# Routing with three chunks in flight and shares in the scattered rows; expert results added into the output by an indirect, accumulating DMA

## The reference

```python
h = x + _attention(_rmsnorm(x, ln1_w), wq, wk, wv, wo)
h = h + _moe(_rmsnorm(h, ln2_w), gate_w, w1, w2, w3)
# _moe:
logits = xf @ gate_w.T
rw, sel = jax.lax.top_k(logits, 2)
rw = jax.nn.softmax(rw, axis=-1)
for e in range(E):
    we = jnp.sum(jnp.where(sel == e, rw, 0.0), axis=-1)
    hid = jax.nn.silu(xf @ w1[e].T) * (xf @ w3[e].T)
    out = out + hid @ w2[e].T * we[:, None]
```

## Time and profile before

| | us |
|---|---|
| median of three runs (3338.06 to 3340.56) | 3339.76 |
| profiled execution, its time | 3338.2 |
| its span | 3336.7 |
| PE busy | 2885.8 (86%) |
| DVE busy | 2463.1 (74%) |
| ACT busy | 1954.1 (59%) |
| POOL busy | 1090.8 (33%) |

### The profile page before, as it was taken

One profiled execution on the slowest core, in us unless ns is written; L12 is line 12 of the kernel. 1 busy time (PEld: TensorE's weight loads), 2 busy tenths in 40 slices (PEclk: granted clock), 3 DMA queues, 4 the chain that ended last, 5 costly groups with the idle time before them and its releaser, 6 DMA issues. The chain is left out here.

```text
span 3336.7 us, 48301 instructions
## 1 busy us (share of the span) xinstructions
PE 2885.8 (86%) x14320; PEld 1233.6 (37%) x14321; DVE 2463.1 (74%) x2747; ACT 1954.1 (59%) x3515; POOL 1090.8 (33%) x652
## 2 busy tenths in 40 slices
PE   5798998889877758999999999999999963899990
PEld 1234434334323431222222222222222252899980
DVE  0599999999998558888888888888888365233323
ACT  3566656655643325888787878787887810344430
POOL 1788779778773450000000000000000036100107
PEclk8899999999998877999999999999999975999995
DMA  1111111111110542111111111111111036111114
GB/s 43 39 51 43 46 54 48 42 54 51 39 44 22 161 144 39 39 37 37 35 39 39 39 40 39 36 32 35 30 38 35 1 118 249 50 47 47 47 41 150
DMA packets 123096, 185.29 MB, mean 56 GB/s; under 512 B 30224, under 2 KB 77968, under 8 KB 122896
## 3 DMA queue, kind: packets, MB, share of 16 engines
q1 hardware_dynamic: 109072, 142.95, 15.0%
q0 software_dynamic: 13824, 39.86, 3.8%
HBM read 138.01 MB, written 44.43 MB: 55 GB/s over the span
## 5 line engine op out<-in xcount | busy, mean ns | idle before, releaser
L1529 DVE TENSOR_REDUCE nmh<-ring 128x2 f32<-128x1024 f32 x1024 | 1196.0, 1219 | 196.1 <-PE ring L1406 195.9
L1387 ACT ACTIVATE prob<-s_ps 128x512 f32<-128x512 f32 x2048 | 1072.9, 602 | 282.5 <-PE s_ps L1427 282.5
L767 DVE TENSOR_TENSOR_SCAN h<-dA,state,bx 128x512 f32<-128x512 f32 x512 | 618.9, 1269 | 124.7 <-ACT dA L606 124.6
L391 POOL TENSOR_TENSOR bx<-u,bb 128x2048 f32<-128x2048 f32 x128 | 578.9, 4527 | 198.1 <-DVE h L767 198.0
L1427 PE MATMUL s_ps<-qs,ks 98*128 98x512 bf16 x2048 | 613.9, 387 | 17.2 <-issue 11.5
L1439 PE MATMUL acc<-prob,vst 128*32 128x512 f32 x4096 | 550.4, 610 | 0.2 <-ACT prob L1387 0.2
L606 ACT ACTIVATE dA<-dt,aneg 128x512 f32<-128x512 f32 x512 | 348.7, 691 | 269.1 <-DVE h L767 269.0
L673 PE MATMUL y_ps<-h,ident 128*128 128x512 f32 x1024 | 495.7, 630 | 0.0
L1406 PE MATMUL ring<-k,q 64*128 64x512 bf16 x2048 | 348.0, 395 | 43.4 <-DMA k<-parts 23.7
L1427 PEld LDWEIGHTS s_ps<-qs,ks 98*128 98x128 bf16 x2048 | 149.3, 97 | 581.4 <-ACT prob L1387 466.3
L673 PEld LDWEIGHTS y_ps<-h,ident 128*128 128x128 f32 x1024 | 208.1, 203 | 234.2 <-issue 228.3
(11 more groups left out here) (222 smaller groups left out, 2634.4 us busy)
## 6 DMA issues: line engine op xcount, KB each, us to landing
bb<-b_rows SPq DMA_DIRECT2D x128, 256.0 KB, 3.1
q<-parts SPq DMA_DIRECT2D x256, 64.0 KB, 2.1
parts<-part POOLq DMA_DIRECT2D x48, 256.0 KB, 3.1
qs<-parts SPq DMA_DIRECT2D x192, 64.0 KB, 2.8
ks<-parts SPq DMA_DIRECT2D x192, 64.0 KB, 2.8
xt<-slots_in POOLq DMA_DIRECT2D x72, 128.0 KB, 2.6
slots_out<-yt SPq DMA_DIRECT2D x72, 128.0 KB, 1.8
k<-parts SPq DMA_DIRECT2D x256, 32.0 KB, 2.0
```

The source lines that it names most:

```text
L391: nc.gpsimd.tensor_tensor(bx[:, n % BR], u[:, b], bb[:, n % RB, None, :].to_broadcast([P, KI, CH]), ALU.mult).then_inc(s_bx, 1)
L767: nc.vector.tensor_tensor_scan(h[:, n % HR, d, :], dA[:, d % 2, :], bx[:, n % BR, d, :], state[:, b, n, d:d + 1], ALU.mult, ALU.add).then_ ...
L1387: nc.scalar.activation(prob[:, k % PR, j, :], s_ps[:, tile % SR, :], ACT.Exp, scale=SC).then_inc(s_exp, 1)
L1529: nc.vector.tensor_reduce(nmh[:, slot, t, 2 * s:2 * s + 2], ring[:, s, :, :], AX.X, ALU.max, negate=True).then_inc(s_free[s], 1)
```

## The change

- `att` is laid out with the token tile ahead of the head, so that PE transposes 128x128 pieces of it directly; `attc` and POOL's copies go.
- The routing block is unrolled over its 8 chunks, with three slots for hc and xr and four for g. On each engine the order is that of the code below. ACT normalizes (Ln, Exp, one scaled copy into g), and PE transposes g itself. The ranks of a chunk follow its own logits.
- A scattered row has 265 elements: 256 of g, 8 with the token's share for each expert, one with the token's number. A row behind a region is zero and points at one of 128 spare rows behind the output.
- The base of the output goes to DRAM at once (`rows_of`), per chunk. The weights of one expert are loaded after each chunk's base. SP writes the zero rows behind the regions.
- All scatters are issued in the one routing block; the second block is gone, and DVE computes the tile table behind its last chunk.
- In the expert stage DVE picks share and token number out of each loaded tile (`pick`), multiplies by the share in `take_y`, and POOL adds the tile into `out` by an indirect DMA with `compute_op=ALU.add`, each after the one before has landed. The stores of yt and the whole combine go.
- `out` has 128 more rows, which the host cuts off.

```diff
 # attention, POOL
-                dst = att[:, bass.ds(n, 1), :, hh * HD:(hh + 1) * HD].rearrange(
-                    "p a (j c) w -> p c (a j) w", c=TT)
+                dst = att[:, :, bass.ds(n, 1), hh * HD:(hh + 1) * HD].rearrange(
+                    "p (j c) a w -> p c (j a) w", c=TT)
...
 # routing, SP
+                def front(c):
+                    wait(sp, s_g, c - FR + 1)
+                    wait(sp, s_bst[r], 16 * (c // FR))
...
+                def keep_base(c):
+                    wait(sp, s_base, c + 1)
+                    sp.dma_start(rows_of(c), xr[:, c % FR]).then_inc(s_bst[c % FR], 16)
...
+                for c in range(FR):
+                    front(c)
...
+                expert_weights(0)
+                for c in range(NC):
+                    keep_base(c)
+                    if c + 1 < NE:
+                        expert_weights(c + 1)
+                    if c + FR < NC:
+                        front(c + FR)
+                sp.wait_ge(s_behind, 1)
+                for e in range(NE):
+                    row = sp.value_load(behind[0:1, e:e + 1], min_val=0, max_val=NE * REG)
+                    sp.dma_start(xg_dram[bass.ds(row, P), :], zero[:, :]).then_inc(s_clear, 16)
 # routing, POOL
+                for c in range(NC):
+                    pool.wait_ge(s_g, c + 1)
+                    pool.wait_ge(s_share, N_SHARE * (c + 1))
+                    pool.wait_ge(s_row, c + 1)
+                    for t in range(TT):
+                        for k in range(2):
+                            nc.gpsimd.indirect_dma_start(
...
+                                in_=g[:, c % GR, t, :], in_offset=None).then_inc(s_sc[c % GR], 16)
 # routing, ACT: normalize(c) is Ln, Exp and four scaled copies hc -> g
+                for c in range(NC):
+                    if c + 1 < NC:
+                        normalize(c + 1)
+                    exponent(c)
+                    if c + 1 < NC:
+                        take_rows(c + 1)
+                    if c + 3 < NC:
+                        take_attention(c + 3)
 # routing, PE
+                for c in range(NC):
+                    logits(c)
+                    if c + 2 < NC:
+                        project(c + 2)
+                    if c + 1 < NC:
+                        turn_rows(c + 1)
+                    if c + 3 < NC:
+                        turn_attention(c + 3)
+                    ranks(c)
 # routing, DVE
+                for c in range(NC):
+                    choose(c)
+                    if c + 2 < NC:
+                        add(c + 2)
+                        moments(c + 2)
+                    shares(c)
+                    if c + 2 < NC:
+                        base(c + 2)
+                    places(c)
...
 # experts, POOL
+                def load(j, slot):
                     row = pool.value_load(first_row[0:1, bass.ds(j, 1)], min_val=0, max_val=NE * REG)
-                    wait_apart(pool, s_xp, j - 3, s_sc)
+                    wait(pool, s_xp, j - 3)
+                    wait(pool, s_pick, j - 3)
                     nc.gpsimd.dma_start(xt[:, slot, :], xg_dram[bass.ds(row, P), :]).then_inc(s_xt[slot], 16)
...
+                def add_to_out(j, slot):
+                    wait(pool, s_yt, j + 1)
+                    wait(pool, s_y, 16 * j)
+                    nc.gpsimd.indirect_dma_start(
+                        out=out[:, :], out_offset=bass.IndirectOffsetOnAxis(ap=token[:, slot:slot + 1], axis=0),
+                        in_=yt[:, slot, :], in_offset=None, compute_op=ALU.add).then_inc(s_y, 16)
+
+                for j in range(NJ):
+                    load(j, j % 4)
+                    if j >= BEHIND:      # BEHIND = 7
+                        add_to_out(j - BEHIND, (j - BEHIND) % 4)
+                for j in range(NJ - BEHIND, NJ):
+                    add_to_out(j, j % 4)
+                pool.wait_ge(s_y, 16 * NJ)
...
 # experts, DVE
+                def pick(j, slot, taken, e):
+                    wait(dve, s_xt[slot], 16 * (taken + 1))
+                    wait(dve, s_y, 16 * (j - 3))
+                    nc.vector.tensor_copy(share[:, slot:slot + 1], xt[:, slot, bass.ds(e + DM, 1)])
+                    nc.vector.tensor_copy(token[:, slot:slot + 1], xt[:, slot, TOK:W]).then_inc(s_pick, 1)
...
                 def take_y(j, q, n):
...
-                    wait(dve, s_y[slot], 16 * taken)
-                    nc.vector.tensor_copy(yt[:, slot, :], o_ps[:, q % 2, 0:DM]).then_inc(s_yt, 1)
+                    wait(dve, s_pick, j - 1)
+                    wait(dve, s_y, 16 * (j - 5))
+                    nc.vector.tensor_scalar(yt[:, slot, :], o_ps[:, q % 2, 0:DM], share[:, slot:slot + 1], None,
+                                            ALU.mult).then_inc(s_yt, 1)
```

More of the change, by code:

```diff
@@ L1677, in moe_stage @@
             s_row = sem("m_row")
+            s_r = sem("m_r")
             s_behind = sem("m_behind")
[L1680 to L1688, removed]
@@ new lines, in _, with take_attention, normalize @@
+                act.wait_ge(s_w, 48)
+                def take_attention(c):
+                    wait(act, s_t1, c + 1)
+                    wait(act, s_wo, c)
+                    nc.scalar.copy(attT[:, :, :], t1_ps[:, :, :]).then_inc(s_aT, 1)
+                def normalize(c):
+                    b, i = where(c)
+                    r = c % GR
+                    wait(act, s_sc[r], 16 * 2 * TT * (c // GR))
+                    nc.scalar.activation(g[:, r, :, TOK], starts[:, tile_of(c):tile_of(c) + TT], ACT.Identity,
+                                         bias=part_no[:, 0:1])
+                    wait(act, s_st, 4 * (c + 1))
+                    nc.scalar.activation(lv[:, :], mv[:, c % 2, :, 1], ACT.Ln, bias=epsc[:, 0:1]).then_inc(s_lv, 1)
+                    wait(act, s_lv, c + 1)
+                    nc.scalar.activation(rs[:, :], lv[:, :], ACT.Exp, scale=-0.5).then_inc(s_rs, 1)
+                    wait(act, s_rs, c + 1)
+                    for t in range(TT):
+                        last = nc.scalar.activation(g[:, r, t, 0:DM], hc[:, c % FR, t, :], ACT.Identity,
+                                                    scale=rs[:, t:t + 1])
+                    last.then_inc(s_g, 1)
@@ L2068, in _, with add @@
             @block.vector
             def _(dve):
+                dve.wait_ge(s_set, SETS)
+                def add(c):
+                    r = c % FR
+                    wait(dve, s_f[r], 32 * (c // FR + 1))
+                    wait(dve, s_wo, c + 1)
+                    for half in range(2):
+                        part = flat(hc[:, r, 2 * half:2 * half + 2, :])
+                        nc.vector.tensor_tensor(part, flat(h_ps[:, 2 * half:2 * half + 2, :]), part, ALU.add
+                                                ).then_inc(s_h, 1)
@@ new lines, in _ @@
+                nc.vector.memset(one[:, :], 1.0)
+                for c in range(2):
+                    add(c)
+                    moments(c)
+                    base(c)
+                for c in range(NC):
[7 more added lines that the diff above has]
+                    places(c)
+                nc.vector.tensor_copy(behind[:, :], count[0:1, :]).then_inc(s_behind, 1)
@@ L2134, in moe_stage @@
             yt = sb3("yt", [P, 4, DM])
+            share = sb3("share", [P, 4])
+            token = sb3("token", [P, 4], U32)
             a_ps = ps3("a_ps", [P, 2, FI])
```

754 lines of the change are left out of this document (292 added, 462 removed).

## The result

The changed kernel takes 3265.1 us (median of 4 runs, 3263.5 to 3266.3) against 3338.9 (4 runs, 3337.5 to 3340.6): ratio 0.9776, interval 0.976 to 0.9791. The forecast was 3226, the range 3200 to 3310. The profiled execution took 3263.52, its span is 3262.0.

What follows compares the result with a forecast made beforehand. Routing bound by row arrival and POOL, experts by PE, combine by a POOL-DVE chain. Span 3336.7 - 39.4 (routing) - 85.1 (combine) + 11 (ring) = 3223.2 us; forecast 3226 us, range 3200 to 3310.

Steps and rivals of the forecast that it cites:

- the likeliest case: The forecast itself, 3226 us, with scatter-add time from 2.7 to 4.1 us and routing gain near 39; chance 0.47.
- the ring: Expert stage: pick, load and scatter-add wait on each other; lap 5.68 us against PE's 5.52, costing 11 us.
- L: Expert stage: time from a scatter-add's start on POOL to the wait it releases, put at 3.84 us.
- an L past 4.2: Expert-stage rival: scatter-adds of 4.2 to 5.4 us set the pace, stage grows 76 us, total 3291; chance 0.25.
- The rest of the lap, 1.84: Expert stage, lap without the scatter-add: pick 0.3 us, release and load 1.24, gap before the next POOL DMA 0.3.
- a clock that falls with PE's gaps: Expert stage, sign of the rival: PE would show idle gaps before `up`, and its clock would fall with them.
- The end, 4.3: After the last yt: the last scatter-add starts once it is ready, 3.9 us to the end; combine's removal saves 85.1.
- Routing, a gain of 39.4: Routing: chunks of 11.7 us, POOL the bound for the last three; last scatter ends at 2797.4, before 2836.85.
- routing gives little: Routing rival: base-row writes and weights hold up chunk loads, so the gain is 16, total 3249; chance 0.13.
- The same 4.9 us behind: Routing's end: the next stage starts 4.9 us after POOL's last scatter, as in the kernel before.
- Both beside the last scatters: Routing's end: SP's eight zero writes, about 10 us, and DVE's table of experts run beside POOL's last scatters.
- The slower case: Expert-stage rival: lap past 7.25 us makes the kernel slower; rows one after another give 3534 us; chance 0.15.

Runs made afterwards that it cites:

- add_first: The changed kernel with POOL's scatter-add of tile j-7 issued ahead of the load of tile j: 3231.2 us, ratio 0.9672.
- late_weights: The changed kernel with the 24 loads of expert weights issued together after the last chunk's loads, instead of three per chunk: 3263.8 us, ratio 0.9768.
- after_again: The changed kernel run once more, unedited, on another chip for a second profile: 3238.2 us, ratio 0.9723.
- pool_zero: The changed kernel with the zero rows scattered by POOL, as before the change, instead of SP's eight writes: 3248.1 us, beside 3240.8 of the changed kernel.
- add_zeros: The changed kernel with POOL's scatter-add ahead of the load and the zero rows written by SP and ACT in turn: 3206.9 us, ratio 0.963.

## Why the prediction was right, and where its sum was off

The kernel is faster by what was named: the combine's 89 us and a part of the routing, less a toll in the expert stage. Of the likeliest case the part on the ring held: it runs just above PE's pace, with L inside its 2.7 to 4.1. Its routing near 39 did not. The measured time is 39 us above the forecast, since routing, experts and end took 18.9, 15.3 and 13.4 us more than the sum had, less 8.8 us of a shorter stretch ahead. It lies in the range by its upper half, which was made for an L past 4.2 and not for these misses; that is luck.

- *Scatter-add, L = 3.84.* Measured 3.93 from start to the pick it releases (2992.72 to 2996.65). The middle between a gather and a gather plus a store came out, but by two errors that nearly cancel: a plain scatter lands in 2.4 us and not in the gather's 2.73, and the addition costs 1.4 where 0.9, and 0.2 for the port, had been put on. The Trainium skill's fit ("DMA: Bandwidth & Descriptors", Anatomy of one DMA) gives 2.3 us by its figures, an estimate by which the ring would have been hidden. That is near the 2.4 of the plain scatter, but doesn't carry over to the accumulating one: 3.8 us to landing. The Trainium skill's statement on the same page (Rules for kernel authors) that such a DMA reads its destination and writes it later is in line with 3.8 with the addition and 2.4 without; the trace doesn't show the two legs apart.
- *The rest of the lap, 1.84.* Measured 2.02: pick 0.22, 0.75 to the load, load 0.74, 0.31 from its end to the add. The load is what was mis-sized: 0.54 from the earlier trace rows, but the ring moves it beside DVE's 0.69 us copy of w1 (2991.60 and 2991.67). Of the 58 loads of the stretch 46 are longer than 0.6 us, and each of these ends 0.11 to 0.14 us after such a copy has ended. Lap 5.95 and not 5.68: 0.43 over PE's 5.52 and not 0.16. A lap priced 5% short made the toll 26 us and not 11, since only the excess over PE's pace counts. The sign that the prediction named with the ring, a clock that falls with PE's gaps, isn't there: it is 0.99 as before.
- *The end, 4.3.* Measured 17.7. The step "the last one starts when the last yt is ready" failed: seven adds are left behind the last load, they start 4.4 to 5.8 us apart, and the last one started 8.7 us after the last yt was ready. The forecast also gave the last add 3.9 to the end of the span; it was 8.5 (3253.52 to 3262.0), 8.6 in add_first and 6.0 without the addition. What fills the 4.7 us behind the last landing isn't shown.
- *Routing, a gain of 39.4.* 20.5 in the first profile, 46 to 47 on two other chips. The model (chunk of 11.7 us, then POOL) was too slow for these: row numbers came 8.9 us apart ((2755.1 - 2693.1)/7) and POOL was the bound throughout. It was too fast for the first chip, where PE's and SP's instructions came late. The rival "routing gives little" had nearly that size, 16, but from traffic of the weights and the written base rows. late_weights speaks against the first, and the gain of 46 to 47 on the other chips, with the same bytes, against both.
- *"The same 4.9 us behind."* 8.5 in after_again (2777.5 to 2786.06), 9.2 in pool_zero; 15.1 in the first profile, where SP's writes ended last. "Both beside the last scatters" was true of SP's eight on the quicker chips (8.9 us) and false on the first (16.9). What makes the 3.6 us above 4.9 was not tested.

The slower case needed L past 5.4, and its price came from rows of one DMA engine one behind the other; the landing of 3.8, 5.0 at most, excludes it.

## What to carry to other kernels

When a change adds waits in a ring, add up the lap and take the issue order out of it before pricing it: swapping two DMAs on one queue gave 31 to 34 us here, and in the expert stage the DMA itself turned out to be free. A queue of serial operations that just keeps pace leaves its backlog at the end, so price the last one by what still stands ahead of it. And the unrolled routing stage differed by 25 us between chips, for a cause that stays open; compare variants on one chip, and by their stages.

## What the runs showed of the hardware

- An indirect DMA from POOL that adds takes 1.59 us of POOL and 3.8 us from issue to landing (3.6 to 5.0) for 128 rows of 1 KB; one that only stores, 1.00 and 2.4. Issued ahead of the load it leaves PE alone: its 400.2 of 405.6 us busy are what they were. Two such adds, each waiting for the landing of the one before, start 4.5 us apart.
- POOL's load of a tile takes 0.54 us of POOL before the change. After it, between 2850 and 3200 us, what counts is when DVE's 0.69 us copy of w1 begins. A load that starts at least 0.2 us before or after the copy's start takes 0.57 to 0.59. One that starts from 0.08 us before to 0.17 after it ends 0.11 to 0.14 us after the copy's end, and so takes 0.64 to 0.90. Most loads of the changed kernel fall so (median 0.74, the first row), and few of add_zeros (0.58, the second):

```profile
L2136 POOL DMA_DIRECT2D xt<-slots_in x58: 568/738/873, 2853.3 to 3195.7; - x58
```
```profile
L2140 POOL DMA_DIRECT2D xt<-slots_in x58: 573/578/896, 2849.5 to 3164.1; - x58
```

- Eight writes of 132.5 KB by SP, each with its address from a register, take 8.9 us to issue on one chip and 16.9 on another.
- PE's instructions in the unrolled routing can come late for no wait that the profile shows, one matmul in 0.7 us for 7 us, with the DMA share at 1.06 and at 0.42 alike, and on two other chips not at all. The granted clock of these ten microseconds is 0.50 (1.2 GHz), after 0.96 in 2695 to 2710 with PE busy 12.6 of 15 us.
